# Rows scattered raw and normalised by VectorE in the expert stage, weights loaded from ScalarE's queue

## What is computed

```python
x = x + tanh(g_xattn[0]) * xattn(layernorm(x), ctx, ctx, mask, wq, bq, wk, bk, wv, bv, wo, bo)
x = x + tanh(g_ffn[0]) * ffn(layernorm(x), gate_w, w1, w3, w2)

def ffn(x, gate_w, w1, w3, w2):              # x is the normalised tensor
    probs = softmax(x @ gate_w)              # 8 experts
    weights, indices = top_k(probs, 2); weights = weights / weights.sum(-1)
    for i in range(8):
        wi = where(indices == i, weights, 0).sum(-1)
        h = silu(x @ w1[i]) * (x @ w3[i])
        out = out + (h @ w2[i]) * wi[..., None]
```

## Time and profile before

| | us |
|---|---|
| runs | 461.36, 457.12, 462.45 (median 461.36) |
| profiled execution | 459.81 |
| its span | 458.1 |
| PE busy in the span | 407.4 (89%) |
| DVE busy | 290.9 (64%) |
| POOL busy | 259.4 (57%) |
| ACT busy | 239.6 (52%) |
| mean granted TensorE clock | 0.972 of full |

### The profile page before, as it was taken

How to read it: one execution, slowest core, us unless ns; L and a number is a source line. 1 busy time by engine, 2 the same in 40 slices (tenths; PEclk the granted TensorE clock), 3 DMA queues, 4 the chain that set the end, 5 groups by cost and what they waited for, 6 DMA issues and landing times.

```text
span 458.1 us, 14422 instructions
## 1 busy us (share of the span) xinstructions
PE 407.4 (89%) x4547; PEld 360.1 (79%) x4548; DVE 290.9 (64%) x786; ACT 239.6 (52%) x564; POOL 259.4 (57%) x312
## 2 busy tenths in 40 slices
PE   2879979999999998997879899988999999999970
PEld 1647658877777776776669799888999999999960
DVE  3876798887888887889546368544444554554420
ACT  2758506667677675766666534233444444444430
POOL 5743554334654737473646568776666665655560
PEclk9989979999999999999999999999999999999995
DMA  7964557457766666485223233334444343333235
GB/s 215 279 123 94 96 96 185 90 105 113 170 147 136 152 134 161 106 216 169 65 69 75 45 52 48 54 67 61 69 70 58 44 54 46 46 47 40 24 29 189
DMA packets 74783, 46.24 MB, mean 101 GB/s; under 512 B 8608, under 2 KB 71490, under 8 KB 74562
## 3 DMA queue, kind: packets, MB, share of 16 engines
q1 hardware_dynamic: 59072, 34.84, 33.2%
q0 software_dynamic: 12272, 8.92, 14.9%
q10 hardware_dynamic: 3392, 1.88, 1.7%
HBM read 18.12 MB, written 14.20 MB: 71 GB/s over the span
## 4 chain that ended last, share of the span: by engine, by line
PE 62%; DMA 9%; issue 7%; DVE 6%; ACT 6%; POOL 4%; ACTq 2%; POOLq 1%; DVEq 0%
PE ps_scores L1612 20%; PE ps_max_scores L1620 10%; DMA sums_scratch<-yt,xg 8%; PE ps_values L897 7%; PE ps_max_scores L853 6%; PE ps_scores L883 5%; PE ps_scores L837 3%; PE ps_max_scores L837 2%; POOL expert_rows_scratch L1328 2%; PE ps_out L921 1%; ACT xn L474 1%; DVE rsplit L1119 1%; ACT w_all L464 1%; DVE qkf L558 1%; POOL sums_scratch L1733 1%
## 5 line engine op out<-in xcount | busy, mean ns | idle before, releaser
L1733 POOL DMA_INDIRECT sums_scratch<-yt,xg x71 | 115.9, 1633 | 66.9 <-DMA sums_scratch<-yt,xg 28.1
L1612 PE MATMUL ps_scores<-xgT,qs 128*128 128x128 f32 x1136 | 141.1, 278 | 5.1 <-ACT xgT L1658 3.8
L1612 PEld LDWEIGHTS ps_scores<-xgT,qs 128*128 128x128 f32 x1136 | 134.1, 194 | 7.1 <-ACT xgT L1658 4.5
L1699 DVE TENSOR_TENSOR qs<-qs,ps_scores 128x512 f32<-128x512 f32 x71 | 48.8, 688 | 88.4 <-PE ps_scores L1612 70.5
L1119 DVE TENSOR_REDUCE rsplit<-ps_max_scores 128x4 f32<-128x512 f32 x128 | 84.8, 685 | 15.0 <-PE ps_max_scores L837 11.2
L1328 POOL DMA_INDIRECT expert_rows_scratch<-xr,pos x64 | 66.4, 1037 | 25.6 <-issue 13.1
L1620 PE MATMUL ps_max_scores<-w_all,qs 128*128 x568 | 75.6, 276 | 2.8 <-ACT yt L1669 2.3
L1620 PEld LDWEIGHTS ps_max_scores<-w_all,qs 128*128 128x128 f32 x568 | 69.0, 192 | 3.8 <-issue 3.6
L1027 ACT ACTIVATE pT<-ps_scores 128x1024 f32<-128x1024 f32 x64 | 62.0, 1022 | 18.1 <-PE ps_scores L837 17.8
L1662 ACT ACTIVATE qs<-ps_scores 128x512 f32<-128x512 f32 x71 | 42.3, 596 | 30.3 <-PE ps_scores L1612 30.3
L1669 ACT ACTIVATE yt<-ps_max_scores,xg 128x128 f32<-128x128 f32 x71 | 26.1, 368 | 60.4 <-PE ps_max_scores L1620 40.4
(11 more groups left out here) (202 smaller groups left out, 527.8 us busy)
## 6 DMA issues: line engine op xcount, KB each, us to landing
qs<-w_all SPq DMA_DIRECT2D x96, 64.0 KB
ks<-w_all SPq DMA_DIRECT2D x96, 64.0 KB
w_all<-in_L_ffn_w_dram SPq DMA_DIRECT2D x24, 256.0 KB
xg<-expert_rows_scratch SPq DMA_DIRECT2D x71, 65.0 KB, 1.9
xs<-in_x_dram SPq DMA_DIRECT2D x4, 512.0 KB, 5.6
sums_scratch<-xs SPq DMA_DIRECT2D x8, 256.0 KB, 4.5
sums_scratch<-yt,xg POOLq DMA_INDIRECT x71, 3.3
expert_rows_scratch<-fill SPq DMA_DIRECT2D x16, 65.0 KB, 2.5
```

Source lines behind the costliest of these rows:

```text
L1612: ins = nc.tensor.matmul(bank[u % 2][:, c * P:(c + 1) * P], w13[:, u % 2, n, c * P:(c + 1) * P], xgT[:], start=True, stop=True)
L1699: nc.vector.tensor_tensor(hidT[:, u % 2], act_s[:, u % 2], ps_b[u % 2], ALU.mult).then_inc(hid_ready, 1)
L1733: pool.indirect_dma_start(out=z_d, out_offset=bass.IndirectOffsetOnAxis(ap=xg_u[:, u, X_IDX:X_IDX + 1], axis=0), in_=yt[:, u % YRING], in_ ...
```

## The change

Raw rows of `xs_all` are scattered instead of normalised copies. The columns of `xs_all` are put in another order: features, mean, then eight logits, whose first three columns are written over with token index, gate and inverse standard deviation once the logits are copied out. A scattered row has 132 numbers instead of 130, and in the expert stage VectorE computes (x + mean) * std^-1 of each tile into a new two-buffer tile `xh`, two tiles ahead; `turn_rows` takes `xh` and waits for it. `norm_rows` and `copy_choice` leave ScalarE, `shift2` leaves GpSimd. Since both copies of a row now come from one place in memory that holds one gate, the four first choices of a group are scattered first; then `second_gates` waits for the landing of these four, writes the second gates, and the four second choices follow. The wait for all eight at a group's end is gone, and each batch issues two scatters. ScalarE issues the 24 weight loads, one in three of four batches, between `load_max` and `copy_attn`. ScalarE's and GpSimd's batches are written out instead of looped (`each_batch`). `choose(LAST)` stands behind tiles 0 to 2 instead of 2 to 4, and `past` and `past_by` have memory of their own, so that a wait for the last scores is gone.

```diff
     CAP = T + P
-    XW = D + 2
-    X_IDX, X_GATE = D, D + 1
-    XE = D + E + 1
-    X_MEAN = XE - 1
+    XE = D + 1 + E
+    X_MEAN = D
+    LOGITS = slice(D + 1, D + 1 + E)
+    X_IDX, X_GATE, X_STD = D + 1, D + 2, D + 3
+    XW = D + 4
...
-        xr = sb("xr", [P, 2, 2, GB, XW])
+        xh = sb("xh", [P, 2, D])
+        past, past_by = (sb(name, [P, max(SURE * E, (NT - SURE) * 2 * E)]) for name in ("past", "past_by"))
...
-        rstd2 = sb("rstd2", [P, GB])
-        shift2 = sb("shift2", [P, GB])
-        xr_u = xr[:].bitcast(U32)
+        var_eps = sb("var_eps", [P, GB])
+        gate2 = sb("gate2", [P, 2, GB])
+        xs_u = xs_all[:].bitcast(U32)
...
         def attend_sync(sp):
-            def load_weights(e, n):
...
-            for e in range(2):
-                for n in range(3):
-                    load_weights(e, n)
             for g in range(2, NG):
...
                     load_half(sp, g, p)
-                    if g >= 3:
-                        for n in (range(0, 1), range(1, 3))[p]:
-                            load_weights(g - 1, n)
-            for n in range(3):
-                load_weights(NG - 1, n)
             for g in range(BEGUN):
...
+            def load_weights(at):
+                e, n = divmod(at.b + 1, GB) if at.b >= GB - 1 else (0, at.b)
+                if n == 3:
+                    return
+                if n == 0:
+                    for p in range(2):
+                        act.wait_ge(qk_loaded[e % 2][p], (e // 2 + 1) * (16 * LOADS))
+                count = 3 * e + n
+                if count >= WEIGHTS:
+                    act.wait_ge(w_loaded[count % WEIGHTS], 16 * (count // WEIGHTS))
+                if n < 2:
+                    to, src = w_sb_all[:, e, n * F:(n + 1) * F], (w1, w3)[n][e]
+                else:
+                    to = w_sb_all[:, e, 2 * F:].rearrange("p (c d) -> p c d", d=D)
+                    src = w2[e].rearrange("(c f) d -> f c d", f=P)
+                act.dma_start(to, src).then_inc(w_loaded[count % WEIGHTS], 16)
             def exps(at, n):
...
-            def norm_rows(r, half):
-                act.wait_ge(r_pool, r.g * 3 + 3)
-                for j in range(half * (GB // 2), (half + 1) * (GB // 2)):
-                    nc.scalar.activation(xr[:, r.u, 0, j, 0:D], xs[:, r.g * GB + j], ACT.Identity,
-                                         bias=shift2[:, j:j + 1], scale=rstd2[:, j:j + 1]).then_inc(xr_ready, 1)
-            def copy_choice(r):
-                act.wait_ge(xr_ready, (r.g + 1) * GB)
-                nc.scalar.copy(xr[:, r.u, 1, :, 0:D], xr[:, r.u, 0, :, 0:D]).then_inc(xr_copied, 1)
             def square(at):
...
                 act.wait_ge(res_done, at.b + 1)
-                nc.scalar.activation(squares[:], xs[:, at.b], ACT.Square, bias=xs_all[:, at.b, X_MEAN:XE],
+                nc.scalar.activation(squares[:], xs[:, at.b], ACT.Square, bias=xs_all[:, at.b, X_MEAN:X_MEAN + 1],
                                      accum_out=var2[:, at.u, at.j:at.j + 1]).then_inc(squared, 1)
...
                     load_max(at.plus(2))
+                if at.b + 1 < E * GB:
+                    load_weights(at)
                 if at.is_past(1) and last.exists():
                     copy_attn(last)
-                if (r := route(at, 2)):
-                    norm_rows(r, 0)
-                if (r := route(at, 3)):
-                    norm_rows(r, 1)
-                    copy_choice(r)
                 if at.is_past(2):
...
                     square(AFTER.plus(-1))
-                elif t in (3, 4):
-                    norm_rows(LAST, t - 3)
-                elif t == 5:
-                    copy_choice(LAST)
                 elif t == 7:
...
                 load_max(At(0, c))
-            batches(act, step)
+            each_batch(step)
             return after, late
...
             def scale_gap(r):
-                dve.wait_ge(r_pool, r.g * 3 + 2)
-                nc.vector.tensor_tensor(ed[:], ed[:], rstd2[:], ALU.mult).then_inc(gap_ready, 1)
+                dve.wait_ge(r_pool, r.g * 2 + 2)
+                nc.vector.tensor_tensor(ed[:], ed[:], xs_all[:, bass.ds(r.g * GB, GB), X_STD], ALU.mult)\
+                    .then_inc(gap_ready, 1)
...
             def late(t):
-                if 2 <= t <= 4:
-                    choose(LAST, t - 2)
+                if t <= 2:
+                    choose(LAST, t)
                 elif t == 6:
...
             def route_std(r):
...
                 stand_alone(pool)
-                pool.tensor_scalar(rstd2[:], var2[:, r.u], 1.0 / D, EPS, ALU.mult, ALU.add).then_inc(r_pool, 1)
-                pool.wait_ge(r_pool, r.g * 3 + 1)
-                pool.tensor_tensor(rstd2[:], rstd2[:], minus_half[:], ALU.pow).then_inc(r_pool, 1)
-                pool.wait_ge(r_pool, r.g * 3 + 2)
-                pool.tensor_tensor(shift2[:], xs_all[:, bass.ds(r.g * GB, GB), X_MEAN], rstd2[:], ALU.mult)\
+                pool.tensor_scalar(var_eps[:], var2[:, r.u], 1.0 / D, EPS, ALU.mult, ALU.add).then_inc(r_pool, 1)
+                pool.wait_ge(choice_step, r.g * (2 * GB + 3) + 1)
+                pool.wait_ge(r_pool, r.g * 2 + 1)
+                stand_alone(pool)
+                pool.tensor_tensor(xs_all[:, bass.ds(r.g * GB, GB), X_STD], var_eps[:], minus_half[:], ALU.pow)\
                     .then_inc(r_pool, 1)
...
-                pool.tensor_copy(xr_u[:, r.u, :, :, X_IDX], idx_f[:]).then_inc(rows_ready, 1)
+                pool.tensor_copy(xs_u[:, bass.ds(r.g * GB, GB), X_IDX], idx_f[:]).then_inc(rows_ready, 1)
                 pool.wait_ge(rows_ready, r.g * 2 + 1)
...
             def place_rows(r):
                 pool.wait_ge(place_step, r.g * 4 + 4)
+                if r.is_past(2):
+                    pool.wait_ge(scattered[r.u], r.half * (2 * GB * 16))
                 stand_alone(pool)
                 pool.tensor_copy(pos[:, r.u], posf[:]).then_inc(pos_ready, 1)
-                pool.tensor_scalar(xr[:, r.u, 0, :, X_GATE], ed1[:], tg[:, 1:2], 0.0, ALU.mult, ALU.add)\
-                    .then_inc(gates_written, 1)
+                gate = xs_all[:, bass.ds(r.g * GB, GB), X_GATE]
+                pool.tensor_scalar(gate, ed1[:], tg[:, 1:2], 0.0, ALU.mult, ALU.add).then_inc(gates_written, 1)
                 pool.wait_ge(gates_written, r.g * 2 + 1)
                 stand_alone(pool)
-                pool.tensor_tensor(xr[:, r.u, 1, :, X_GATE], xr[:, r.u, 0, :, X_GATE], ed[:], ALU.mult)\
-                    .then_inc(gates_written, 1)
+                pool.tensor_tensor(gate2[:, r.u], gate, ed[:], ALU.mult).then_inc(gates_written, 1)
+            def second_gates(r):
+                pool.wait_ge(scattered[r.u], r.half * (2 * GB * 16) + GB * 16)
+                stand_alone(pool)
+                pool.tensor_copy(xs_all[:, bass.ds(r.g * GB, GB), X_GATE], gate2[:, r.u]).then_inc(second_ready, 1)
...
                     pool.wait_ge(gates_written, r.g * 2 + 2)
-                    pool.wait_ge(xr_copied, r.g + 1)
+                    pool.wait_ge(rows_ready, r.g * 2 + 1)
+                    stand_alone(pool)
+                if GB in rows:
+                    second_gates(r)
+                    pool.wait_ge(second_ready, r.g + 1)
                     stand_alone(pool)
                 for n in rows:
-                    j, k = n // 2, n % 2
+                    k, j = n // GB, n % GB
                     pool.indirect_dma_start(
                         out=rows_d, out_offset=bass.IndirectOffsetOnAxis(ap=pos[:, r.u, k, j:j + 1], axis=0),
-                        in_=xr[:, r.u, k, j], in_offset=None).then_inc(scattered[r.u], 16)
+                        in_=xs_all[:, r.g * GB + j, 0:XW], in_offset=None).then_inc(scattered[r.u], 16)
...
                         place_rows(sent)
-                    scatter(sent, (range(0, 2), range(2, 5), range(5, 7), range(7, 8))[at.j])
-                if at.j == 3 and sent.exists() and (not at.known or sent.g + 2 < NG):
-                    pool.wait_ge(scattered[sent.u], sent.half * (2 * GB * 16) + 2 * GB * 16)
-                    stand_alone(pool)
+                    scatter(sent, (range(0, 2), range(2, 4), range(4, 6), range(6, 8))[at.j])
...
-        past, past_by = (ks[0][:].bitcast(F32).rearrange("p h t -> p (h t)")[:, i * GT * H // 4:(i + 1) * GT * H // 4]
-                         for i in range(2))
-        assert SURE < NT and (NT - SURE) * 2 * E <= GT * H // 4
+        assert SURE < NT
         plan_step = sem("plan_step")
...
             else:
-                dve.wait_ge(scored, (B - GB) * NB)
                 for n in range(2 * part - 4, 2 * part - 2):
...
             def turn_rows(t, u, turn):
-                pe.wait_ge(xg_loaded[u], turn * 16 + 16)
-                nc.tensor.transpose(ps_x(t), xg[:, u, 0:D], ident[:]).then_inc(xg_turned, 1)
+                pe.wait_ge(xh_ready, t + 1)
+                nc.tensor.transpose(ps_x(t), xh[:, u % 2], ident[:]).then_inc(xg_turned, 1)
...
+            def norm_rows(t, u, turn):
```

(10 more changed lines are left out.)

46 lines of the change are left out of this document (19 added, 27 removed).

## The result

The changed kernel takes 476.86 us (median of 473.33 to 481.43, four runs) beside 461.56 for the kernel before: ratio 1.033, 95% interval 1.022 to 1.043, 15.3 us slower. The profiled execution's span is 475.9 us against 458.1.

What follows compares the result with a forecast made beforehand. TensorE was taken to bound attention and steady expert tiles, GpSimd's sends the chain between. Terms -0.5 + 2.2 - 0.2 + 0.8 = +2.3 us on the middle, 460.6, gave 462.9 us (bounds 459.8 to 465.1; range with rivals 456.0 to 467.0).

Steps and rivals of the forecast that it cites:

- two falls of the clock: Slower rival's larger case: TensorE's clock falls in the holes ahead of both up(0) and down(0), giving 466.3 us.
- The weight loads: Attention: ScalarE's issue of each load, median 0.39 us, hides in its wait of about 1 us ahead of copy_attn; cost nothing.
- Attention's relief: Attention: 18.9 us off ScalarE; a quarter of TensorE's 2.1 us wait for pT goes, -0.5 us (bounds 0 and -2.1).
- Rival 2: Faster, chance 0.24: in attention both TensorE waits at the values matmul go, -4.4 and -2.1 us, giving 456.9 us.
- The seam: First expert tiles: xh delays up(0) by 1.1 us and down(0) by another 1.1, first send +2.2 us (bounds 1.1, 2.4).
- rival 1: Slower, chance 0.22: TensorE's clock falls in the new holes at the first tiles, 1.7 us each; one fall 464.6 us.
- The third part: First expert tiles: tile 2's xh stands behind the product and weights' copy, another 1.1 us before down(0).
- VectorE's step: Expert tiles: one more VectorE operation, the xh, in each of 71 tiles, 0.24 us (bounds 0.18 and 0.29).
- The steady tiles: Expert stage: VectorE's tile goes from 1.40 to 1.64 of 2.8 us, done two tiles ahead, so it costs nothing.
- GpSimd's terms: GpSimd among the first tiles: shift2 removed, -0.2 us; second_gates ahead of the last group's fifth scatter, +0.8 us.
- The delay of the first send: Expert stage: GpSimd's sends form the chain, so the first send's 2.2 us delay moves everything after it.

Runs made afterwards that it cites:

- 11: The changed kernel without VectorE's normalising, TensorE turning the raw rows, weight loads still on ScalarE: 470.4 us (462.08 to 474.88).
- 12: The changed kernel without VectorE's normalising and with the weight loads back on SyncE: 461.35 us, 1.001 of the kernel before.
- 17: The changed kernel with the weight loads back on SyncE, all else as changed: 467.41 us beside 461.13 for the kernel before, 1.011.
- the tiny transfers: The changed kernel with weight loads on SyncE and 24 unused 2 KB transfers issued by ScalarE in their place: 496.44 beside 484.16 us (1.024); repeated, 503.97 us (1.036).
- experiment 2: The kernel before with only the weight loads moved to ScalarE, and ScalarE's batches written out for that: 493.76 us beside 484.16, 1.017.
- the copy alone: The kernel before with VectorE copying each tile's rows into xh where the changed kernel normalises: 464.54 us beside 459.56, 1.011.
- experiment 4: The kernel before with ScalarE's and GpSimd's batches written out instead of looped, nothing else: 486.87 us beside 484.16, 1.008.

## Why the prediction was wrong

I forecast +2.3 us and measured +15.3. No rival as I put it gives this: two falls of the clock ended at 466.3.

**The weight loads: this step failed.** "An issue of 0.39 us hides in that", and "I cost them at nothing". They cost 4 to 9 us of the 15.3 by experiments 11 and 12, and 9 by the changed kernel and 17, on two chips, and the reasoning was off twice. First, the cover of about 1 us ahead of `copy_attn` was the issue of `load_max`, 0.72 us in 0.79; the tiny transfers show what that is worth, 1.3 to 1.5 us in the first seven batches. Second, I did not weigh the 12 KB of the maxima, which batch 3 got 9.2 us after their issue. With loads on SyncE b0-b7 is 34.5 to 34.8 us (once 35.9); tiny transfers on ScalarE make it 36.1 and 36.2, real loads 37.1 to 40.1 in the changed kernel with and without normalising, though only 36.0 in experiment 2. The Trainium skill, "DMA: Bandwidth & Descriptors", section "Queues, rings and completion order", says that each of SyncE and ScalarE has one queue with a ring on each of the 16 DMA engines, that a ring is worked off in order, and that a DMA engine takes turns between queues. By that rule a load from ScalarE's own queue could stand in front of the small transfer. The trace does not agree for the one that took 9.2 us: its queue had nothing older left from 81.2 us on, and it moved at 87.4. The same page, section "Issuing engines are not separate DMA queues", says that starting DMAs on several engines only saves sequencer time; here the first seven batches differ by 2.3 to 5.6 us, more than the 1.3 to 1.5 of the issues.

What makes the small transfer late is not shown. Order within the queue is refuted for the worst case. The moment of the loads changed together with their issuer and is an untested rival: SyncE issues the first six between 68.0 and 72.3 us and the next at 101.1, ScalarE issues them at 72.0, 76.1, 81.1, 86.4, 94.9 and 99.8, beside SyncE's loads of 64 KB for the next batches. A kernel in which SyncE issues the loads at ScalarE's moments would tell the two apart.

**Attention's relief, forecast -0.5.** ScalarE's wait did shrink by 1.7 us (2.1 to 0.4), but without normalising and with loads on SyncE the total is 1.001 of before: nothing is won on balance. Rival 2, which wanted 3.7 us less, is refuted by the same run.

**The seam, forecast +2.2, measured +5.3.** The places were right: `turn(0)` behind L1190, tile 2's rows ahead of `down(0)`. The sizes fell short. `up(0)` itself came 5.07 us behind batch 30's output (3.62 before), 1.45 later where 1.1 was forecast. Then rival 1 came true once: 3.78 us instead of 2.05, 1.7 us more, and some 0.6 in the three rows behind it (0.63, 0.42 and 2.24 us where the earlier trace rows and the same place before have 0.38, 0.27 and 2.05). I had given it 0.22 as an alternative, when the forecast itself made a hole of 2.3 us, as long as the 2.2 of the earlier trace rows. It should have been a term. The third part, 1.26 us of waiting for tile 2's rows and an idle of 0.74 ahead of `down(0)` in place of 0.45, is the remaining 1.6 us; I had 1.1.

**VectorE's step, forecast 0.24 us, measured 0.34** (mean of 38: 342 ns), above my upper bound of 0.29 from an operation of the same shape, which reads PSUM and no scalar operands. The steady tiles were costed at nothing and lost 1.3 us, in a few tiles only.

**GpSimd's terms, forecast +0.6 together:** 0.9 us from the first send to output 30 in the profiled execution, in a column that runs from 88.6 to 90.8 among kernels with the same second gates, so it is not settled; no wait for the landing shows. The delay of the first send did carry through to the end, as forecast: the copy alone lost 5.2 us at the seam and 5.0 in the total. VectorE's 5.0 us and the loads' 9 us at most make 14; the rest, 1.3 us or more, has no experiment of its own. That the forecast's places at the seam and the carry-through were right does not make its small total less wrong: most of what was missed lies in attention, at a term put at nothing.

## What to carry to other kernels

Before moving DMAs to another engine, list which small transfers that engine already issues, how long before their need, and what else moves at the new moment; here a 12 KB transfer landed up to 9.3 us after its issue when the loads were moved beside it, for a reason that stays open. Idle time ahead of an instruction in a profile of busy times may be the issue of a DMA, so read the queue's own rows before counting it as cover. When a forecast makes a hole in TensorE's work as long as one after which the clock already fell in the same trace, the slower matmuls belong in the sum. A step handed to another engine can want one tile more of lead than its bare time says: here three tiles instead of two, the first ones ahead of the first weights, took 467.41 us to 462.38, level with before.

## What was not expected

Two chips ran the unchanged kernel at 484 us where others took 459 to 462. The excess lies in attention behind batch 7: b7-b30 is 147.2 us in experiment 4 against 120.8, all else within 1 us. The waits there, 60 to 262 us of experiment 4, have rows such as these; "remote" is a wait whose end the trace does not name:

```profile
DVE rsplit L1123 <- remote: 19.1, 9, 2.4
ACT attnT L1040 <- remote: 17.7, 5, 3.8
POOL vst L1289 <- remote: 10.2, 9, 2.0
```

The kernel before on the first chip has two such rows, 2.0 and 2.3 us. What these pauses are stays open. So does why the loads' place was worth only 0.7 and 3.4 us in the total on those two (501.54 to 500.81, 502.51 to 499.08). In the first seven batches, ahead of the pauses, it shows there too: 38.1 us to 34.5 and 37.1 to 34.8. That pauses in TensorE's path leave the small transfer more time to land would fit, and was not tested.
